# A new order inside the slots of a two-expert feed-forward and scan-attention pipeline: gates as Tanh, rows normalised by ScalarE, routing rows normalised later

## What is computed

```
x = x + 0.5 * ffn0(norm(x))      # feed-forward with 8 low-rank experts, the best 2 per token
x = x + attn0(norm(x))           # gated scan, then a small MLP
x = x + 0.5 * ffn0(norm(x))      # the same feed-forward again
x = x + 0.5 * ffn1(norm(x))      # one of 8 experts per token, by routing
x = x + attn1(norm(x))           # softmax attention
x = x + 0.5 * ffn1(norm(x))

ffn0:  t = rms(x) * norm_w;  weights = top-2 softmax of t @ gate.T
       h1 = t @ w1.T + 2 * lora1_e(t);  h3 = t @ w3.T + 2 * lora3_e(t)
       act = silu(h1) * h3;  out = sum_e weights_e * (act @ w2.T + 2 * lora2_e(act))
attn0: i, f, o = sigmoid(h @ Wi + bi), sigmoid(h @ Wf + bf), sigmoid(h @ Wo + bo)
       two first-order scans over the sequence with f and i; z = x + o * num / den
       z + (leaky(ln(z) @ W1 + b1))**2 @ W2 + b2
```

## Time and profile before

| | |
|---|---|
| median of 3 runs | 1050.17 us (1050.05 to 1051.02) |
| the profiled execution | 1054.69 us, of which the span from first to last instruction 1053.0 us |
| PE busy | 980.6 us, 93% of the span |
| DVE, ACT, POOL busy | 711.2, 507.9, 500.1 us (68, 48, 47%) |
| mean granted TensorE clock | 0.992 |

### The profile page before, as it was taken

The page is one execution under the profiler, slowest core; times in us unless marked ns, Lnnn a source line. Parts: engine busy times, 40 slices in busy tenths (PEclk is TensorE's granted clock), DMA queues, the critical chain, the costliest instruction groups (busy, mean ns, idle before and its releaser), DMA issues. The chain is left out here.

```text
span 1053.0 us, 15574 instructions
## 1 busy us (share of the span) xinstructions
PE 980.6 (93%) x4429; PEld 669.9 (64%) x4429; DVE 711.2 (68%) x2140; ACT 507.9 (48%) x1039; POOL 500.1 (47%) x485
## 2 busy tenths in 40 slices
PE   3999999999999999999999999899988999889993
PEld 2766667656565665656566656477864667648873
DVE  5787779788786877879797776445543667634542
ACT  3433454655646556564453332144534777515451
POOL 3456555554535545354654655524451155423443
PEclk9999999999999999999999999999999999989997
DMA  6069000000000000000000002146534000015651
GB/s 181 1 284 415 3 1 1 1 1 1 1 0 2 0 1 1 1 0 1 12 3 9 11 11 71 39 137 197 166 94 140 1 22 22 22 42 178 194 174 34
DMA packets 42900, 65.12 MB, mean 62 GB/s; under 512 B 7153, under 2 KB 25121, under 8 KB 40640
## 3 DMA queue, kind: packets, MB, share of 16 engines
q1 hardware_dynamic: 37824, 55.59, 16.1%
q0 software_dynamic: 4992, 8.54, 2.4%
HBM read 37.20 MB, written 28.74 MB: 63 GB/s over the span
## 5 line engine op out<-in xcount | busy, mean ns | idle before, releaser
L362 PE MATMUL bank<-split 128*128 128x512 f32 x416 | 206.9, 497 | 7.8 <-DVE ud L1267 4.1
L364 PE MATMUL bank<-split 128*128 128x512 f32 x416 | 165.2, 397 | 0.0
L363 PE MATMUL bank<-split 128*128 128x512 f32 x416 | 164.8, 396 | 0.0
L863 ACT ACTIVATE sil<-bank 128x512 f32<-128x512 f32 x128 | 76.2, 595 | 116.0 <-PE bank L364 115.2
L1644 POOL TENSOR_TENSOR gsum<-act 128x512 f32<-128x512 f32 x64 | 84.9, 1327 | 81.5 <-DVE act L1203 81.4
L421 PE MATMUL bank<-act,a 128*128 128x512 f32 x256 | 117.6, 592 | 0.0
L362 PEld LDWEIGHTS bank<-split 128*128 128x128 f32 x416 | 79.5, 191 | 48.8 <-issue 17.4
L1199 DVE TENSOR_TENSOR act<-bank,sil 128x512 f32<-128x512 f32 x128 | 87.8, 686 | 17.2 <-PE bank L364 14.2
L363 PEld LDWEIGHTS bank<-split 128*128 128x128 f32 x416 | 79.9, 192 | 28.3 <-issue 18.6
L688 PE MATMUL bank<-xlT,e 128*128 128x256 f32 x368 | 91.2, 392 | 5.1 <-ACT xlT L1068 2.7
L1203 DVE TENSOR_TENSOR act<-act,wT 128x512 f32<-128x512 f32 x128 | 91.7, 716 | 4.4
(11 more groups left out here) (283 smaller groups left out, 1957.6 us busy)
## 6 DMA issues: line engine op xcount, KB each, us to landing
e<-e_dram SPq DMA_DIRECT2D x92, 256.0 KB, 3.1
rows_in<-yw SPq DMA_DIRECT2D x17, 1056.0 KB, 17.8
xin<-rows_in SPq DMA_DIRECT2D x46, 132.0 KB, 3.0
x<-rows_out SPq DMA_DIRECT2D x8, 256.0 KB, 4.7
rows_in<-yw,slot_i POOLq DMA_INDIRECT x64, 2.3
rows_out<-ob,ids POOLq DMA_INDIRECT x46, 2.3
out<-ob,ids POOLq DMA_INDIRECT x46, 2.4
act<-b_dram SPq DMA_DIRECT2D x2, 256.0 KB, 3.1
```

The lines of the kernel that those rows point to most:

```text
L362: mm(dst, w[0], m[0], start=start, stop=False, **more)
L363: mm(dst, w[0], m[1], start=False, stop=False, **more)
L364: return mm(dst, w[1], m[0], start=False, stop=stop, **more)
L863: af(sil[(k - 1) % 2][:, :], bank[BH1[STEPS[k - 1][0] % 2]][:, :], ACT.Silu).then_inc(silu_done.sem, 1)
```

## The change

Nothing is added to or taken from PE's work. The products are the same; the order is another.

- PE: `pre_T` and `logits` come early in the slot. `value(1)` comes before `a_back`. The three masks move forward by a step. `a_gate(0..3)` no longer stand together at the end but after `down(0)`, after `down(1)`, after `up(1)`, and between the two halves of `value(0)`. `up(0)` and `up(1)` stand one step earlier. The middle products of the attention's MLP use bank BV, and the routing's transposes BSIDE.
- ACT: Sigmoid(y + b) becomes Tanh(0.5 y + 0.5 b), and a Copy with scale 0.5 and bias 0.5 in place (`gates_done`). `half` holds half the biases, made once. `f_norm` is here now, as four Identity ACTIVATEs at the end of the slot before. `r_norm(r_pre)` stands in the middle of a slot for slots 10 to 16; before, that normalisation was at the end of the slot before.
- DVE: `f_norm` is gone. The two `top2`, `a_add`, `f_stats`, `masked` and `act(8)` stand earlier, `first_values` stands behind `a_scans`.
- POOL: `f_scale` has a second small product, `nb_f`. `up_low(0)` stands ahead of `total(2)` and `total(3)`.

The two last down products, `down(2)` and `down(3)`, stay the last calls of their own slot, and `SLOTS` is as it was.

```diff
@@ POOL: f_scale
                     pool.tensor_tensor(sc_f[n % 2][:, 1, :], sc_f[n % 2][:, 0, :], neghalf[:, 0:T], ALU.pow).then_inc(rstd_f.sem, 1)
+                    pool.wait_ge(*rstd_f(n, 1))
+                    pool.tensor_tensor(nb_f[n % 2][:, :], sc_f[n % 2][:, 1, :], mv_f[n % 2][:, :], ALU.mult).then_inc(rstd_f.sem, 1)
@@ ACT: f_norm, in place of DVE's
+                def f_norm():
+                    n = s.stat
+                    if n is None:
+                        return
+                    act.wait_ge(*rstd_f(n))
+                    act.wait_ge(*ynT_f(n - 1))
+                    for t in range(T):
+                        last = af(yn_f[:, t, :], xc(n)[:, t, :], ACT.Identity, bias=nb_f[n % 2][:, t:t + 1], scale=sc_f[n % 2][:, 1, t:t + 1])
+                    last.then_inc(normed_f.sem, 1)
@@ ACT: gates
-                def a_gates():
+                def a_gate(i):
                     n = s.a_gate
                     if n is None:
                         return
+                    dst = (gi, gf, go)[i]
                     act.wait_ge(*oa_ready(n - 1))
-                    for i, (dst, bias) in enumerate(((gi, bif[:, 0:1]), (gf, bif[:, 1:2]), (go, vecs[:, 5:6]))):
-                        act.wait_ge(*gates_ready(n, i + 1))
-                        af(dst[:, :], bank[BSIDE][:, :], ACT.Sigmoid, bias=bias).then_inc(gates_saved.sem, 1)
+                    act.wait_ge(*gates_ready(n, i + 1))
+                    af(dst[:, :], bank[BSIDE][:, :], ACT.Tanh, bias=half[:, i:i + 1], scale=0.5).then_inc(gates_saved.sem, 1)
+                    act.wait_ge(*gates_saved(n, i + 1))
+                    af(dst[:, :], dst[:, :], ACT.Copy, scale=0.5, bias=0.5).then_inc(gates_done.sem, 1)
...
@@ POOL: the slot's order
-                total(2)
-                total(3)
                 up_low(0)
+                total(2)
+                total(3)
                 up_low(1)
```

More of the change, by code:

```diff
@@ L109, in build @@
         mv_f = [sb(f"mv_f{i}", [P, T]) for i in range(2)]; sc_f = [sb(f"sc_f{i}", [P, 2, T]) for i in range(2)]
+        nb_f = [sb(f"nb_f{i}", [P, T]) for i in range(2)]
         yn_f = sb("yn_f", [P, T, P])
@@ L621, in fill @@
                         keep_busy(count)
-                h(1, 1); h(3, 1)
+                h(1, 1)
+                pre_T()
+                h(3, 1)
                 a_T()
                 h(1, 2)
+                logits()
+                if q == 0:
+                    up(0); up(1)
+                h(3, 2)
                 a_den()
-                h(3, 2)
-                pre_T()
+                value(1, range(J))
                 a_back()
-                value(1, range(J))
                 h(1, 3)
```

153 lines of the change are left out of this document (73 added, 80 removed).

## The result

The changed kernel takes 1055.58 us in the median (1054.18 to 1057.05), 1.0052 times the kernel before, with a 95% interval of 1.0037 to 1.0066. It is slower, where 1045.5 was forecast and a range of 1034 to 1052. A second set of twelve executions gave 1054.29 us and 1.0037 (1.0022 to 1.0051). The profiled execution took 1056.43 us, with a span of 1054.7 us from the first to the last instruction.

What follows compares the result with a forecast made beforehand. PE, working in 93% of the span, was taken as the bound, so only its waits counted. Gains of 17.2 us less losses of 12.5 gave 4.7, turning 1050.2 into 1045.5 us, range 1034 to 1052.

Steps and rivals of the forecast that it cites:

- 0.25 was taken: Slots with gates: PE reaches a_out at 13.4 and z is there at about 13.6; 0.25 us lost a slot.
- 0.5 was taken: End of slots with gates: POOL's sums late for down(2) and down(3); 0.5 us lost a slot, bounds 0 and 1.0.
- 9.4 + 2.1 gained: Slots 3 to 10: gate waits vanish, 9.4 us; up(0) no longer waits for the last mask, 0.26 a slot.
- 2.0 + 4.0 lost: Slots 3 to 10: new waits for z at a_out, 2.0 us, and for POOL's sums at down(2) and down(3), 4.0.
- 1.5 was forecast: Slots 13 and 14: shorter up(1) waits for masked(0) and 0.26 a slot at up(0), less about 0.4 for late sums.
- 1.7 and 0.6: Start: 1.7 us lost, bounds 0.7 and 3; slot 0: 0.9 lost to late sums, against 0.26 gained at up(0).
- term of 0.75 for the second chunk: Slot 0: PE has pre_T right behind the first step, but ACT reaches that chunk's f_norm after all splits; 0.75 us lost.
- 0.9 us a slot: Slots 0 to 2 and 12: PE is ready for down(2) and down(3) before POOL's sums; 0.9 us lost a slot.
- The 1.0 for waits too small for a row: Added to the gains: 1.0 us for waits of 0.1 to 0.3 us, given no place.
- C: Rival, chance 0.10: DVE and POOL hold each other up, 1.1 us more a slot over 14 slots; slower, 1061 us.
- B: Rival, chance 0.14: gate waits return at down(2), down(3) and up(1), about 1 us a slot; 1050 us.

Runs made afterwards that it cites:

- e10_best2: Changed kernel with POOL's sums before the first two splits outside slots 6 to 10, first chunk's normalisation on DVE, z early in slots 10 and 11: 1041.52 us.
- e1_z11: Changed kernel, with DVE taking second_values and a_mix ahead of top2(1) in slot 11 alone: 1055.47 us, ratio 1.0052 to the kernel before.
- second profiles: The kernel before and the changed kernel, both unchanged, profiled once more: last value product of the slots starts at 654.1 and 657.9 us.
- e3_start: Changed kernel with the first chunk's normalisation alone back on DVE: 1054.09 us, ratio 1.0037 to the kernel before.
- e2_pool: Changed kernel with POOL's order as before, total(2) and total(3) ahead of up_low(0): 1043.57 us, ratio 0.9942 to the kernel before.
- e6_leaky_short: Changed kernel with DVE's leaky step on 8 of 512 columns, the rest of that step left out: 1049.0 us, ratio 0.998 to the kernel before.
- e11_second_chunk: e10_best2 with the second chunk's normalisation on DVE too, behind the second mask: 1042.51 us, ratio 0.9931 to the kernel before.
- e8_fnorm_dve: Changed kernel with the FFN's rows normalised by DVE again at its slot's end, all chunks but the first: 1113.41 us, ratio 1.0609 to the kernel before.

## Why the prediction was wrong

**Right: a full slot. Wrong: slots 3 and 4.** The gates' waits are gone, a full slot takes 44.2 (forecast 43.8 to 44.5), z costs 0.24 in slot 9 (0.25 was taken), and POOL's sum 0.25 (0.5 was taken). The prediction's terms for slots 3 to 10 are 9.4 + 2.1 gained and 2.0 + 4.0 lost, net 5.5; measured are 4.3. By slots 0.56 was forecast for each and 1.0 more in slot 5; slots 6 to 9 gained 0.6 to 0.9 each and slot 5 2.1, but slot 3 lost 0.3 and slot 4 0.8. The prediction took slot 9 for all eight. In slot 3 before, the second gate starts right behind `value`, and in slot 4 0.25 us late, so there was little to gain; and in the changed kernel slot 3 waits 0.9 for POOL's sum, and slot 4 waits 0.8 for it and 0.8 for `x` of DVE's L1305, a wait that no term names. That the eight together came within 1.2 us is in part luck, since the full slots and slot 5 gained more than forecast and covered half of what these two lost. Slots 13 and 14 gained 1.2, where 1.5 was forecast.

**Wrong above all: slot 11, by a term that was read off another slot.** The prediction says of it: "In slot 11 the routing product stands there instead and waits 0.9, but it waited as long before." So the wait for z was put at nothing in this slot. Both halves fail. Before, the routing product did not wait; what waited in slot 11 were PE's transposes, 0.7 us for the denominator (`denc`). And the new wait is not 0.9 but 2.2. Counted from PE's first product, z is done in slot 9 at 14.3 us and PE is there at 14.2 (the prediction had 13.6 and 13.4, and so the right margin). In slot 11 PE is there at 13.0, 1.2 us sooner: the transposes of `yn_a` are not in that slot (0.35), and L523 stands ahead of `h(3, 3)`, where the other slots' L536 stands behind it (0.7). And z is done at 15.1, 0.8 us later. 0.24 + 1.2 + 0.8 is the wait of 2.2. The first part was to be had from the list alone. The step that failed is the transfer of one slot's margin to a slot with another list.

Why z is later than in slot 9 is seen in DVE's queue at the head of slot 11. Before, the six small routing steps took 0.5 us together. After, they take 2.3, with POOL at work beside them:

```profile
468.50 0.87 DVE L1423 TENSOR_TENSOR invs<-sc_r 128x4 f32<-128x4 f32 x1
469.29 0.16 DVE L1424 TENSOR_SCALAR rf<-sc_r 128x4 f32<-128x4 f32 x1
469.36 1.26 DVE L1428 TENSOR_SCALAR yw<-mv_r 128x4 f32<-128x4 f32 x1
```

```profile
468.07 1.28 POOL L1720 TENSOR_TENSOR oaT<-num,go 128x512 f32<-128x512 f32 x1 [1.16 <-DVE num L1373]
469.30 1.29 POOL L1640 TENSOR_TENSOR split<-tT,split 128x512 fp32r<-128x512 f32 x1
```

Both long ones end when POOL's product ends, at 469.4 and 470.6. They are 4 columns wide. (Most of the way of z to its place has another cause, the order: both top-2 now stand ahead of it, 1.6 and 1.9 us.)

**Not foreseen: the clock.** Slot 11 with only a wait of 0.85 for z is 42.9 us (e10_best2). The changed kernel has 47.8 and 49.4. Of the 4.9 and 6.5 more, 1.3 is the longer wait for z and 1.2 the two late sums (what they cost in slot 12). The clock's share is 1.6 and 3.2: e1_z11's slot at full clock, 46.1, had 2.1 us of waits where this has 2.2, so 46.2 is the slot without the fall. That is about half of the 3.4 and 6.8 us for which the clock is low. Some 0.7 is left over, 0.3 of it the later Silu of slot 12, the rest not traced. The prediction priced a wait at its own length; here, with the fall behind it, it went with up to two and a half times that.

**The start: one term too low, the sum about right.** The first Silu comes 2.4 us later and slot 0 is 1.1 longer by the second profiles, against 1.7 and 0.6. The term of 0.75 for the second chunk was half of what it should be. ACT runs all four normalisations ahead of the table load for the first Silu, in the changed kernel:

```profile
27.71 1.63 ACT L891 ACTIVATE yn_f<-x,nb_f,sc_f 128x128 f32<-128x128 f32 x4
29.36 1.28 ACT L866 ACT_TABLE_LOAD   x1
30.65 0.60 ACT L866 ACTIVATE sil<-bank 128x512 f32<-128x512 f32 x1
```

With them moved away the Silu came 1.6 us sooner. The rest is 0.5 for the first chunk (e3_start) and about 0.3 that is left for POOL's added product, which no run isolates. The first transpose started at 10.2 us, forecast 10.

How long slot 0 is depends on when the clock rises. PE's first fp32r products of slot 0 run at the lower level. When it rises, the starts of fp32r products change from 0.43 apart to 0.23. (The clock column of the windows has no record of this stretch and prints 1.00.) The kernel before, first and second profile:

```profile
31.14 0.63 PE L364 MATMUL bank<-split 128*128 128x512 f32 x1
31.57 0.50 PE L362 MATMUL bank<-split 128*128 128x512 f32 x1
31.91 0.39 PE L363 MATMUL bank<-split 128*128 128x512 f32 x1
```

```profile
28.75 0.63 PE L364 MATMUL bank<-split 128*128 128x512 f32 x1
29.18 0.48 PE L362 MATMUL bank<-split 128*128 128x512 f32 x1
29.50 0.40 PE L363 MATMUL bank<-split 128*128 128x512 f32 x1
```

It rises at 31.8 and 29.4 us, and PE runs at half speed until then. 2.4 us at half speed are the 1.2 us by which slot 0 of the two differs. In the changed kernel it rises at 32.1 and 32.8. By the first profiles, where the rise is at almost the same time, the change costs 2.2 us up to the first Silu of slot 1, where 1.7 + 0.6 was forecast; by the second, where the rises are 3.4 us apart, it costs 3.5. Whether a later start also makes the clock rise later was not settled.

**Slots 0 to 2 and 12.** 0.9 us a slot was taken for the late sums; they cost 1.07 in slots 0 and 1 and 1.2 in 11 and 12. The sign and cause were right and e2_pool took all of it back. The prediction was to be wrong "if slots 0 to 2 grow by more than 1 us": slots 1 and 2 grew by 1.0 and 0.9, and slot 0 by 1.1 or not at all, as the clock had it.

**The ledger.** By the second profiles slots 11 to 14 came out 5.0 us worse than forecast (6.7 by the first), the start with slots 0 to 2 1.9 worse (0.5 by the first, the clock's rise making the difference), and slots 3 to 10 1.2 worse (1.0). The 1.0 for waits too small for a row was never seen as such. Without it, and counted slot by slot, the forecast is -4.0; slot 15 came out 0.3 better. -4.0 + 5.0 + 1.9 + 1.2 - 0.3 is +3.8 us, by which the slots' part grew. Behind the slots nothing stands out (395.4 and 394.7 us, against 397.7 and 395.0 before). The medians moved by 5.4 and 3.2 us in the two sets.

**The rivals.** C forecast the sign, and its mechanism is real: sums at 1.46 in place of 1.33, three DVE groups up by 40 us. Its price and place were wrong. It put 1.1 us on each slot, and slots 6 to 9 came out 0.1 to 0.3 us better than in my own sum; it costs where a queue with no margin stands behind, at z in slot 11 (e6_leaky_short gained 5 to 7 us, in slots 6 to 10 as well). B, waits that only move, holds for POOL's order: sums first or splits first, each makes the other late, and e2_pool shows which slots want which.

Of the shared interface, POOL and DVE take turns here by whole instructions, as the rows of e6_leaky_short and e11_second_chunk show. The Trainium skill says the same: by its page "SBUF — State Buffer" (SBUF: two separate sides) whichever starts first, a GpSimd instruction or a VectorE instruction in a two-port mode or with two SBUF inputs, gets the shared pair for its whole instruction and the other is blocked until then; against two SBUF inputs that holds for a GpSimd instruction that reads SBUF. The rows of e6_leaky_short agree: 1.23 us for 8 columns beside a sum. In place of the slowdown ratios of the earlier trace rows, such a turn of POOL, up to 1.3 us by the rows here, would have stood ahead of each such DVE instruction in the count.

## What to carry to other kernels

When an order is changed in a pipeline, make the list of waits for each kind of slot that has another list of stages, not for the fullest one only: the full slots came out to 0.3 us each, and slots 3, 4 and 11, with other lists, carried most of the miss. Measure a slot on the engine that bounds it: by the first Silu, which a table load held up before, slot 3 seemed to gain 0.9 us and had lost 0.3. Order the queue of a secondary engine by when its consumer needs each piece and when its input is there; both putting z last (2.2 us lost in slot 11) and putting it first everywhere (2.3 us lost in each of slots 4 and 5) were wrong; chosen by slot, together with POOL's order and the first chunk's place, it made a kernel 8 us below the one before. Do not lay instructions of DVE with two operands in SBUF beside POOL's products ahead of something that PE waits for.

## What the runs showed of the hardware

- A DVE instruction with two operands in SBUF, or a TENSOR_SCALAR on rows in SBUF, lasted until POOL's running product had ended, whatever its size: 8 columns took 1.23 us, 4 columns 0.87 and 1.26, four normalisations of 128 columns 4.12 (1.11 in the earlier trace rows). Products that read a bank were not held (of the changed kernel's 128 L1220, 54 lay for over nine tenths of their time beside a product of POOL, and none took over 0.69), nor were the statistics of z (0.28 to 0.30 each, all 32 beside POOL). POOL waits in turn behind long ones: 1.27 became 1.72 beside a leaky step and 2.2 beside a scan.
- The granted clock fell to 1.2 GHz behind waits of 1.3 to 2.2 us in slot 11, and once behind two of 0.9 and 1.2, for 3.4 or 6.8 us; with the same instructions it did not fall in another execution. It did not fall behind the wait of 1.6 in the earlier trace rows (1.00 from 581 to 590 us). In e8_fnorm_dve it fell at the waits of 4.6 us in slots 6 to 11, behind one of 2.5 in slot 5 and one of 2.2 in slot 12, and not behind 2.4 in slot 4 and 2.2 in slot 13. What makes the difference was not settled.
- PE's first fp32r products of slot 0 ran at half speed. The clock rose at 31.8 and at 29.4 us in two executions of the same kernel, which is worth 1.2 us, and between 29.4 and 33.9 us in all profiles but that of e8_fnorm_dve (37.2, where PE stood 2.1 us idle in slot 0 for its rows).
- ACT's table load took 1.28 us, and what stood behind it started 0.01 to 0.02 us after its end (once 0.06), 18 times up to 661 us in the kernel before.
